# A four-layer graph network in split fp32: twelve SBUF tensors laid 32 bytes off the 64-byte multiples

## The chip, the cores and the metric

The kernel runs on one core of one Trainium2 chip. The metric is the device time of one execution in microseconds (us). The profile gives one execution, instruction by instruction, on the core's engines: PE (TensorE matrix products) and PEld (its loads of the stationary operand), DVE (VectorE), ACT (ScalarE), POOL (GpSimd) and SP (which issues the transfers).

## What is computed

Thirty-two graphs of 256 nodes with 256 features go through four layers, each followed by a residual sum and a layer norm. The parts that matter here:

```python
def _L0_gnn_ref(x, in_mat, out_mat, w3_w, ...):      # in_mat = out_mat = adj
    for _ in range(3):
        a_in = jnp.einsum('nm,bmd->bnd', in_mat, h)
        av = jnp.concatenate([a_in, a_out], axis=-1)
        z = sigmoid(_lin(av, w3_w, w3_b) + _lin(h, u3_w, u3_b))
        r = sigmoid(_lin(av, w4_w, w4_b) + _lin(h, u3_w, u3_b))
        hv = tanh(_lin(av, w5_w, w5_b) + _lin(r * h, u5_w, u5_b))
        h = (1.0 - z) * h + z * hv
def _L1_gnn_ref(s, adjacency, Wq, Wk, Wv):           # relation, masked and normed, times values
    rel = adjacency.T[None] * jnp.einsum('bnd,bmd->bnm', q, k)
    return jnp.einsum('bnm,bmd->bnd', rel / norm(rel, axis=2, keepdims=True), v)
def _L2_gnn_ref(x, adj, weight, bias):   # (adj x) W + b
def _L3_gnn_ref(x, adj, weight, bias):   # (D^-1/2 adj D^-1/2)(x W) + b
x = _layernorm(x + L0(x)); x = _layernorm(x + L1(x)); x = _layernorm(x + L2(x)); x = _layernorm(x + L3(x))
```

## The kernel before

Two graphs are one pair; there are 16 pairs. A full tile is 128 partitions x 2 x 512 numbers of four bytes: features on the partitions, the nodes of both graphs along the row. Every operand of a product is kept as two tensors of type fp32r, the rounded value (`_hi`) and the rest (`_lo`), and each product is three: high by high, high by low, low by high. So each matrix is a `Split` of two tensors.

The products come in two shapes. In the **512-column** products a weight matrix is the stationary operand (128 of its columns) and 512 columns of a state tile move through the array: `base` (u3T), `reset` (w4T), `update` (w34T), `candidate_mixed` (w5T), `candidate_reset` (u5T). In the **256-column** products a matrix or tile of 256 columns moves:

- `mix` and `mix_nodes`: `adjT` (or `norm_adjT`) moves, the stationary operand is 128 columns of a node-major state (`hf_node`, `hb_node`, `b_a`).
- `convolve`: `w2s` or `w3s` moves, `b_rh` is stationary.
- `keys`: the split sum (`sum_hi`, `sum_lo`) moves, `wqk` is stationary.
- `values`: `wvT` moves, the split sum is stationary.
- `relate`: the keys (`b_rh`) move, the split sum is stationary.
- `attend`: the values (`v_hi`, `v_lo`) move, the split relation (`rel_hi`, `rel_lo`) is stationary.

In the profile a product is written out<-moving,stationary, so `b_ps<-sum_hi,wqk_lo` has the high half of the sum moving over `wqk_lo`. Each product is a load of 128 stationary columns (PEld) and the matmul (PE). Line 515 is the call in the helper `matmul`, line 510 that in `product`.

The order of work on every engine is written out by hand: a part for the start, a loop body that PE, DVE, ACT, POOL and SP run 13 times, and an ending in which the last two pairs run side by side. A body works on two recurrence steps of the front pair (`f_`, `hf_`), the third step of the pair before it (`b_`, `hb_`), and that pair's other three layers. Engines meet through semaphores. The last pair (`last_pair`) has no tensors of its own: its sum stands in `hb_feat_hi` and `hb_feat_lo`, its relation in `hf_node_hi` and `hf_node_lo`, its values in `hf_feat_hi` and `hf_feat_lo`.

Tensors are laid out in SBUF in the order in which they are allocated, each start rounded up to 32 bytes. In the built program of before, all operands of all products start at multiples of 128 bytes: `adjT_hi` at 16512, `wqk_hi` at 49280, `b_rh_hi` at 155264, `sum_hi` at 190080, `rel_hi` at 214656. Slices of them start at multiples of 512 bytes from there. Some small tensors and `bias_out` (at 64928, read by DVE at line 1715) already stand 32 bytes off a multiple of 64.

The lines that allocate what the change moves:

```python
        def split_matrix(name):
            return Split(sb(name + "_hi", [P, C, D], F32R), sb(name + "_lo", [P, C, D], F32R))

        adjT = split_matrix("adjT")
        norm_adjT = split_matrix("norm_adjT")
```

Of the kernel before, what the change touches and what calls it, by code (L numbers as in the profile page):

```python
# [21 lines left out]
P = 128  # L22
F32 = mybir.dt.float32
F32R = mybir.dt.float32r
# [136 lines left out]
def build(nc, x, adj, w3_w, w3_b, u3_w, u3_b, w4_w, w4_b, w5_w, w5_b, u5_w, u5_b, wq, wk, wv,  # L161
          l2_w, l2_b, l3_w, l3_b, out):
    B, N, D = x.shape
    C = N // P
    G = 2
    T = G * N
# [9 lines left out]
    with ExitStack() as ctx:  # L176
        def sb(name, shape, dt=F32):
            return ctx.enter_context(nc.sbuf_tensor(name, shape, dt))
# [5 lines left out]
        def split_matrix(name):  # L184
            return Split(sb(name + "_hi", [P, C, D], F32R), sb(name + "_lo", [P, C, D], F32R))

        adjT = split_matrix("adjT")
        norm_adjT = split_matrix("norm_adjT")
        w34T = split_matrix("w34T")
        w4T = split_matrix("w4T")  # L190
        w5T = split_matrix("w5T")
# [1 line left out]
        u5T = split_matrix("u5T")  # L193
        wvT = split_matrix("wvT")
        wqk = split_matrix("wqk")
        w2s = split_matrix("w2s")
        w3s = split_matrix("w3s")

        ident = sb("ident", [P, P])
        adj_nat = sb("adj_nat", [P, C, N])  # L200
# [47 lines left out]
        def nodes(name, dt=F32):  # L248
            return sb(name, [P, G, C, D], dt)

        main = Layers(sb, sem, "b", back, per_graph, input_t, s_input_t, 0,
                      (sb("sum_hi", [P, C, T], F32R), sb("sum_lo", [P, C, T], F32R)), nodes("normed"), nodes("result"),
                      (nodes("v_hi", F32R), nodes("v_lo", F32R)), (nodes("rel_hi", F32R), nodes("rel_lo", F32R)),
                      sb("sq_sum", [P, G, N]), True)


# [1981 lines left out]
```

## Time and profile before

| | us |
|---|---|
| median of 3 runs | 1224.64 |
| lowest and highest | 1224.62, 1224.92 |
| the profiled execution | 1224.91 |
| its span, first to last instruction | 1223.1 |
| outside the span | 1.8 |

The profiled execution stands 0.27 us over the median of the runs. Its mean granted TensorE clock was 0.998 of full speed. The profile's page gives busy time by engine, 40 slices of the span, the chain of work that ended last and the costliest groups of instructions; views of the trace give instructions in order of time, groups by line and tile, and busy time by stretch. A matmul's recorded length includes its way through the array and overlaps the next one's, so what a matmul costs in a run is the distance from its start to the next start, not its length.

### The profile page before, as it was taken

To read this page: it belongs to the slowest core of one execution; us is meant where nothing else is said; L and a number is where in the kernel's file an instruction comes from. 1 tells how busy PE (TensorE), PEld (TensorE's weight loads), DVE (VectorE), ACT (ScalarE), POOL (GpSimd) and SP (SyncE) were. 2 spreads that over 40 slices of the span, in tenths; PEclk is the share of its full clock that TensorE was granted. 3 is DMA by queue.
4 is the path that set the end of the run, shared out by engine and by line. 5 is a ranking of instruction groups with operands and counts; after the bars stand their busy time and mean duration, and the time that the engine had idled before them with its cause. 6 is when DMAs were issued, how large, how long until landed. Compare 5 with 4: busy or idle time off the path is not lost.

```text
span 1223.1 us, 21243 instructions
## 1 busy us (share of the span) xinstructions
PE 1207.9 (99%) x7454; PEld 1089.1 (89%) x7454; DVE 1003.4 (82%) x2220; ACT 657.5 (54%) x1179; POOL 192.8 (16%) x447
## 2 busy tenths in 40 slices
PE   9999999999999999999999999999999999999997
PEld 7789899898998989899898998989989898998896
DVE  7689788897878978788887888978789787886799
ACT  5455555555555555555555555555555555555542
POOL 1002021110211102012020211102111021120122
PEclk9999999999999999999999999999999999999999
DMA  6020221303113030120402213031130311300001
GB/s 207 18 84 21 63 77 35 103 0 86 51 34 103 0 103 34 46 91 1 119 17 53 84 34 103 0 86 51 34 103 0 103 34 42 95 1 35 1 2 35
DMA packets 105021, 66.93 MB, mean 55 GB/s; under 512 B 65690, under 2 KB 98468, under 8 KB 104996
## 3 DMA queue, kind: packets, MB, share of 16 engines
q1 hardware_dynamic: 104784, 66.08, 18.2%
q0 software_dynamic: 192, 0.52, 0.2%
q8 instruction: 15, 0.25, 0.1%
q14 instruction: 10, 0.08, 0.0%
q10 hardware_dynamic: 20, 0.01, 0.0%
HBM read 35.13 MB, written 23.07 MB: 48 GB/s over the span
## 4 chain that ended last, share of the span: by engine, by line
PE 97%; DVE 2%; POOL 0%; ACT 0%; issue 0%; DVEq 0%; POOLq 0%
PE b_ps L515 41%; PE f_ps L515 31%; PE f_ps L510 15%; PE b_ps L510 7%; PE f_ps L677 1%; PE b_ps L741 1%; PE b_ps L559 0%; PE f_ps L1052 0%; DVE b_stats L1678 0%; DVE f_stats L1678 0%; DVE f_gate L1694 0%; PE b_ps L574 0%; DVE hf_feat L1706 0%; DVE hf_feat L1694 0%; DVE normed L1694 0%
## 5 line engine op out<-in xcount | busy, mean ns | idle before, releaser
L423 POOL TENSOR_TENSOR b_var_eps<-b_moments,eps 128x2 f32<-128x2 f32 x120 | 34.9, 290 | 913.1 <-DVE b_moments L1685 913.0
L1115 ACT ACTIVATE f_cand<-f_ps,bias_c 128x512 f32<-128x512 f32 x66 | 45.6, 691 | 86.0 <-PE f_ps L515 84.3
L425 POOL TENSOR_TENSOR b_rstd<-b_var_eps,neg_half 128x2 f32<-128x2 f32 x120 | 88.2, 735 | 9.4
L1063 ACT ACTIVATE b_rh_hi<-b_ps 128x512 fp32r<-128x512 f32 x90 | 53.7, 596 | 65.5 <-PE b_ps L515 65.5
L1103 ACT ACTIVATE f_gate<-f_ps,bias_r 128x512 f32<-128x512 f32 x66 | 45.4, 688 | 70.7 <-PE f_ps L515 70.7
L1063 ACT ACTIVATE b_a_hi<-normed 128x512 fp32r<-128x512 f32 x60 | 37.9, 632 | 61.3 <-DVE normed L1694 61.3
L515 PE MATMUL f_ps<-adjT_hi,hf_node_hi 128*128 128x256 f32 x264 | 67.3, 287 | 0.5 <-DVE adjT_lo L1481 0.5
L515 PE MATMUL f_ps<-adjT_lo,hf_node_hi 128*128 128x256 f32 x264 | 66.1, 283 | 0.0
L1720 DVE TENSOR_TENSOR b_rh_lo<-b_ps,b_rh_hi 128x512 fp32r<-128x512 f32 x90 | 61.4, 682 | 4.6 <-ACT b_rh_hi L1063 4.4
L1577 DVE TENSOR_TENSOR f_cand<-f_z,f_cand 128x512 f32<-128x512 f32 x66 | 45.5, 689 | 23.0 <-ACT f_cand L1115 23.0
L1561 DVE TENSOR_TENSOR f_gate<-f_gate,hf_feat 128x512 f32<-128x512 f32 x66 | 44.8, 680 | 20.2 <-ACT f_gate L1103 20.2
L1063 ACT ACTIVATE f_a_hi<-f_ps 128x512 fp32r<-128x512 f32 x66 | 39.0, 592 | 40.5 <-PE f_ps L515 40.5
L1555 DVE TENSOR_TENSOR b_a_lo<-b_ps,b_a_hi 128x512 fp32r<-128x512 f32 x30 | 19.4, 687 | 49.2 <-ACT b_a_hi L1063 49.2
L1111 ACT ACTIVATE f_z<-f_ps,bias_z 128x512 f32<-128x512 f32 x66 | 45.1, 685 | 26.6 <-PE f_ps L510 26.6
L1555 DVE TENSOR_TENSOR f_a_lo<-f_ps,f_a_hi 128x512 fp32r<-128x512 f32 x66 | 44.9, 682 | 14.0 <-ACT f_a_hi L1063 14.0
L1182 ACT ACTIVATE result<-result,b_shift,b_rstd 128x256 f32<-128x256 f32 x56 | 30.8, 597 | 46.2 <-POOL b_shift L431 46.2
L1063 ACT ACTIVATE hf_feat_hi<-hf_feat 128x512 fp32r<-128x512 f32 x64 | 38.8, 626 | 25.1 <-DVE hf_feat L1641 22.2
L515 PE MATMUL f_ps<-hf_feat_hi,u3T_hi 128*128 128x512 f32 x132 | 52.0, 394 | 0.1
L515 PE MATMUL f_ps<-f_a_hi,w4T_hi 128*128 128x512 f32 x132 | 51.8, 393 | 0.0
L515 PE MATMUL f_ps<-hf_feat_hi,u3T_lo 128*128 128x512 f32 x132 | 51.8, 392 | 0.0
L515 PE MATMUL f_ps<-f_a_hi,w4T_lo 128*128 128x512 f32 x132 | 51.6, 391 | 0.0
L510 PE MATMUL f_ps<-f_a_hi,w34T_hi 128*128 128x512 f32 x132 | 51.5, 390 | 0.0
(340 smaller groups left out, 4335.7 us busy)
## 6 DMA issues: line engine op xcount, KB each, us to landing
x_front<-in_x SPq DMA_DIRECT2D x16, 512.0 KB, 4.0
x_blocks<-in_x SPq DMA_DIRECT2D x60, 128.0 KB, 2.9
input_t<-hf_feat SPq DMA_DIRECT2D x15, 512.0 KB, 2.9
turn_sum<-normed SPq DMA_DIRECT2D x14, 512.0 KB, 2.7
result<-turn_sum SPq DMA_DIRECT2D x56, 128.0 KB, 2.8
turn_f<-f_gate SPq DMA_DIRECT2D x14, 512.0 KB, 2.7
f_z<-turn_f SPq DMA_DIRECT2D x56, 128.0 KB, 2.8
out<-result SPq DMA_DIRECT2D x14, 512.0 KB, 3.2
```

Of the source, the lines that this page charges most:

```text
L423: pool.tensor_tensor(Y.var_eps[:, g], Y.moments[:, g, :, 1], eps[:], ALU.add).then_inc(Y.s_var, 1)
L425: pool.tensor_tensor(Y.rstd[:, g], Y.var_eps[:, g], neg_half[:], ALU.pow).then_inc(Y.s_rstd, 1)
L510: last = pe.matmul(bank, s, m, start=start and i == 0, stop=stop and i == len(terms) - 1, skip_group_check=True)
L515: return pe.matmul(bank, s, m, start=start, stop=stop, skip_group_check=True)
L1063: return act.activation(dst, src, ACT.Copy)
L1103: act.activation(L.gate[:, k], L.ps0[:, k], ACT.Sigmoid, bias=bias_r[:, k:k + 1]).then_inc(L.s_r, 1)
L1111: act.activation(L.z[:, k], L.ps0[:, k], ACT.Sigmoid, bias=bias_z[:, k:k + 1]).then_inc(L.s_z, 1)
L1115: act.activation(L.cand[:, k], L.ps1[:, k], ACT.Tanh, bias=bias_c[:, k:k + 1]).then_inc(L.s_tanh, 1)
L1555: dve.tensor_tensor(L.a_lo[:, k], L.ps1[:, k], full(L.a_hi[:, k]), ALU.subtract).then_inc(L.s_a_lo, 1)
L1561: dve.tensor_tensor(L.gate[:, k], L.gate[:, k], L.state.feat[:, k], ALU.mult).then_inc(L.s_rh, 1)
L1577: dve.tensor_tensor(L.cand[:, k], L.z[:, k], L.cand[:, k], ALU.mult).then_inc(L.s_zc, 1)
L1720: dve.tensor_tensor(lo[:, g], src, full(hi[:, g]), ALU.subtract).then_inc(done, 1)
```

## The change

Twelve tensors (four split matrices, the split sum and the split relation) are allocated behind a new tensor of 32 bytes, and a second one of 32 bytes follows them, so that all that comes behind stands where it stood relative to 64. The order of instructions on all five engines is word for word that of before, with the same shapes; what differs is addresses alone.

In the built program after, these twelve tensors start 32 bytes off a multiple of 64: `adjT_hi` (173728), `adjT_lo`, `norm_adjT_hi`, `norm_adjT_lo`, `w2s_hi`, `w2s_lo`, `w3s_hi`, `w3s_lo`, `sum_hi` (190112), `sum_lo`, `rel_hi` (198304), `rel_lo`. All the other operands of products keep their place relative to 64.

```diff
-        adjT = split_matrix("adjT")
-        norm_adjT = split_matrix("norm_adjT")
...
-        w2s = split_matrix("w2s")
-        w3s = split_matrix("w3s")
...
+        shift_32 = sb("shift_32", [P, 8])
+        adjT = split_matrix("adjT")
+        norm_adjT = split_matrix("norm_adjT")
+        w2s = split_matrix("w2s")
+        w3s = split_matrix("w3s")
+        sum_split = sb("sum_hi", [P, C, T], F32R), sb("sum_lo", [P, C, T], F32R)
+        rel_split = nodes("rel_hi", F32R), nodes("rel_lo", F32R)
+        shift_back = sb("shift_back", [P, 8])
+
         main = Layers(sb, sem, "b", back, per_graph, input_t, s_input_t, 0,
-                      (sb("sum_hi", [P, C, T], F32R), sb("sum_lo", [P, C, T], F32R)), nodes("normed"), nodes("result"),
-                      (nodes("v_hi", F32R), nodes("v_lo", F32R)), (nodes("rel_hi", F32R), nodes("rel_lo", F32R)),
+                      sum_split, nodes("normed"), nodes("result"),
+                      (nodes("v_hi", F32R), nodes("v_lo", F32R)), rel_split,
                       sb("sq_sum", [P, G, N]), True)
```

So in each 256-column product of the first fifteen pairs exactly one of the two operands stands off by 32 bytes: the moving one in `mix`, `mix_nodes`, `convolve` and `keys`, the stationary one in `values`, `relate` and `attend`. In the 512-column products neither does, nor in the last pair's `keys`, `values`, `relate` and `attend`.

## Rows read from the trace of the kernel before

**Rows 1.** The page: engines' busy time, granted clock, and the chain that ended last.

```profile
PE 1207.9 (99%) x7454; PEld 1089.1 (89%) x7454; DVE 1003.4 (82%) x2220; ACT 657.5 (54%) x1179; POOL 192.8 (16%) x447
...
PEclk9999999999999999999999999999999999999999
...
PE 97%; DVE 2%; POOL 0%; ACT 0%; issue 0%; DVEq 0%; POOLq 0%
```

**Rows 2.** Busy time by stretch: start and length, then each engine (x instructions), clock, DMA.

```profile
0.00:54.00 54.00, 49.23 (x255) 41.80 (x256) 39.06 (x75) 29.50 (x49) 4.25 (x15) 0.97 0.42 127
...
572.65:647.00 74.35, 74.35 (x462) 67.19 (x461) 61.64 (x136) 40.94 (x76) 11.91 (x28) 1.00 0.19 56
...
1093.10:1223.10 130.00, 119.61 (x770) 108.13 (x768) 104.74 (x253) 57.26 (x102) 23.30 (x48) 0.99 0.05 17
```

**Rows 3.** Chain that ended last, in order of time: start us, length us, what.

```profile
592.20 5.44 PE f_ps L515 x24
605.80 7.19 PE b_ps L515 x60
652.93 5.47 PE b_ps L515 x24
658.40 5.44 PE b_ps L510 x24
```

**Rows 4.** PE in order of time, from 512 to 256 columns: start us, length us, instruction.

```profile
602.92 0.39 PE L510 MATMUL f_ps<-f_a_hi,w34T_hi 128*128 128x512 f32 x1
...
605.19 0.62 PE L515 MATMUL f_ps<-f_rh_lo,u5T_hi 128*128 128x512 f32 x2
605.64 0.28 PE L515 MATMUL b_ps<-sum_hi,wqk_hi 128*128 128x256 f32 x1
605.75 0.28 PE L515 MATMUL b_ps<-sum_hi,wqk_lo 128*128 128x256 f32 x1
605.87 0.28 PE L515 MATMUL b_ps<-sum_hi,wqk_hi 128*128 128x256 f32 x1
...
607.07 0.28 PE L515 MATMUL b_ps<-sum_hi,wqk_hi 128*128 128x256 f32 x1
```

**Rows 5.** PE in order of time, 512-column matmuls right behind a 256-column run.

```profile
629.23 0.40 PE L510 MATMUL f_ps<-f_a_hi,w34T_hi 128*128 128x512 f32 x1
629.46 0.40 PE L510 MATMUL f_ps<-f_a_lo,w34T_hi 128*128 128x512 f32 x1
629.70 0.39 PE L510 MATMUL f_ps<-f_a_hi,w34T_lo 128*128 128x512 f32 x1
...
630.62 0.28 PE L515 MATMUL b_ps<-adjT_hi,b_a_hi 128*128 128x256 f32 x1
```

**Rows 6.** PEld in order of time: weight loads of eight 128-column transposes, then the next.

```profile
644.61 0.90 PEld L677 LDWEIGHTS f_ps<-ident,hb_feat 128*128 128x128 f32 x8
645.47 0.19 PEld L515 LDWEIGHTS b_ps<-w3s_hi,b_rh_hi 128*128 128x128 f32 x1
```

**Rows 7.** Groups by line: out<-moving,stationary, x count | busy us, mean ns | idle before.

```profile
L515 PE MATMUL f_ps<-adjT_hi,hf_node_hi 128*128 128x256 f32 x264 | 67.3, 287 | 0.5 <-DVE adjT_lo L1481 0.5
...
L510 PE MATMUL f_ps<-f_a_hi,w34T_lo 128*128 128x512 f32 x132 | 51.3, 389 | 0.0
...
L515 PE MATMUL b_ps<-sum_hi,wqk_lo 128*128 128x256 f32 x120 | 30.1, 283 | 0.0
...
L515 PE MATMUL f_ps<-hb_feat_hi,wqk_hi 128*128 128x256 f32 x8 | 2.0, 283 | 0.0
...
L510 PEld LDWEIGHTS f_ps<-f_a_hi,w34T_lo 128*128 128x128 f32 x132 | 24.8, 188 | 5.3
...
L515 PEld LDWEIGHTS b_ps<-sum_hi,wqk_lo 128*128 128x128 f32 x120 | 23.0, 191 | 0.6
```

**Rows 8.** One tile each: count, duration ns min/median/max, first and last start us.

```profile
L1715 DVE TENSOR_TENSOR b_ps<-normed,bias_out x60: 674/694/700, 105.4 to 1212.9; 128x512 f32<-128x512 f32 x60
L1724 DVE TENSOR_TENSOR sum_lo<-b_cand,sum_hi x30: 676/686/690, 78.0 to 1158.2; 128x512 fp32r<-128x512 f32 x30
```

**Rows 9.** DVE and PE in order of time at a hand-over in a body (`mix_nodes` to `convolve`).

```profile
642.89 0.69 DVE L1720 TENSOR_TENSOR b_rh_lo<-b_ps,b_rh_hi 128x512 fp32r<-128x512 f32 x1
643.27 0.28 PE L515 MATMUL b_ps<-w3s_hi,b_rh_hi 128*128 128x256 f32 x1
...
644.23 0.28 PE L515 MATMUL b_ps<-w3s_hi,b_rh_lo 128*128 128x256 f32 x1
```

## Prediction, made before the changed kernel was run

> **What bounds the kernel now.** The first view is the page's: PE is busy in 99% of the span, its clock is granted in full in every slice, and the chain that ended last lies 97% on PE [rows 1]. That busy share alone says little, since matmuls overlap in the records. So the second view is busy time by stretch: in one loop body of 74.35 us PE is busy in all of it and never waits, DVE is busy in 61.64 us (83%), ACT in 40.94 [rows 2]. Thirteen such bodies are 967 of the 1223.1 us. PE is the bound, and no other engine holds it up there; only the start and the ending, with 49.23 busy of 54.00 and 119.61 of 130.00 us, have gaps [rows 2].
>
> The third view is what a matmul costs by its distance to the next. The chain's pieces give it best: 24 matmuls of 512 columns take 5.44 us, 226.7 ns each, and 60 of 256 columns (`keys`, `values(0)` and `relate`) take 7.19 us, 119.8 ns each [rows 3]. By single starts it is the same: ten 512-column steps from 602.92 to 605.19 are 2.27 us, ten 256-column steps from 605.87 to 607.07 are 1.20 us [rows 4]. Here the two shapes do not agree. At 226.7 ns for 512 columns, 256 columns should take 113.3 ns. They take 120, so 6.7 ns of each are not moving columns.
>
> **Where the 6.7 ns sit.** The first 256-column matmul behind a 512-column run takes only 0.11 us (605.64 to 605.75), the next ones 0.12 [rows 4]. It has the same operands, the same addresses modulo 64 and the same shape; what differs is how its stream lies in time against the load of the next weights. The other side of the same thing: 512-column matmuls right behind a 256-column run start at 629.23, 629.46 and 629.70 and six of them take 1.39 us, 232 ns each and up to 0.24, against 226.7 later [rows 5]. The weight load is recorded at 191 ns under 256 columns and 188 under 512, the 256-column matmul at 283 [rows 7]. So a load and a stream that run together can cost more or less, at the same addresses, by their relative position, and the steady state of a 256-column run is the dear one. Could it be the weight load alone that sets 120 ns? Eight loads for 128-column transposes start within 0.86 us, 107.5 ns apart [rows 6]. These are a transpose's loads, so this bounds the load rather than measures it, but it leaves room under 113.3.
>
> **The change part by part.** Instructions, their order and their shapes are the same on all engines; no wait, transfer or queue moves. What can change is the time of an instruction that reads or writes one of the twelve tensors.
>
> *PE.* The 256-column matmuls number 4224: three groups like the first of x264, 27 groups of x120, 24 groups of x8 in the last pair [rows 7]. Of the last pair's, twelve groups (96 matmuls) touch no moved tensor. In the other 4128 the two operands were in step modulo 64 and are now 32 bytes apart. That is an untried relation: no product in the trace has it, so it has to be bounded. Below: the load at 107.5 ns, 12.5 ns less per matmul, if the shift also took away what both shapes pay now [rows 6]. Above: the dearest step of the 512-column rows, 0.24 us, 13 ns over 226.7 [rows 5]; on the same footing a 256-column step would cost 113.3 + 13 = 126, 6 ns more than now. The nearest row is the 0.11 us step, since it is the same matmul with another relative position [rows 4]. A shift by 32 bytes is eight numbers of the stream, 8 x 0.443 = 3.5 ns of it at the 512-column rate (226.7 / 512). The relation moves by a few ns, as it does between the first matmul of a run and the rest. I take 113.3 for that reason. It is a choice: the row shows that position matters, not that this position is the good one.
>
> Not all 4128 pay 6.7 ns now. The first one or two of a run are already cheap, and some sit behind a wait. I count nine in ten, 3,700: 3,700 x 6.7 ns = **24.8 us**.
>
> *512-column products.* None of their operands moves, and they are 2880, fifteen groups of x132 and fifteen of x60, such as the one shown [rows 7]. What they pay behind a 256-column run, (232 - 226.7) x 6 = 32 ns [rows 5], should go if that run ends in the cheap relation. With about ten such places in each of some 15 passes this is at most 4.8 us. I take half, **2.4 us**.
>
> *DVE, ACT and the transfers.* DVE writes `sum_lo` at 32 bytes off now. The trace has such a case: `bias_out` stands off already, and the DVE operation that reads it takes 694 ns against 686 for `sum_lo` with the same shape, and that difference includes a PSUM destination [rows 8]. At 8 ns for the 60 `sum_lo` and `rel_lo` writes it is 0.5 us in all, on an engine that is idle for 12.7 us of each body [rows 2]; zero. On ACT it is likewise off the path.
>
> *What is late next.* A body would shrink by about 1.8 us to 72.6, with DVE at 61.64, 85%. Hand-overs inside it: `b_rh_lo` is written by 643.58 and first read at 644.23, 0.65 us of slack [rows 9]. Between the matmuls that feed it and that read lie some 20 of 256 columns, which shrink by 0.13 us. So in the body the whole gain stays. In the ending, where PE lacks 10.4 of 130 us [rows 2], about 600 of the matmuls stand, worth 3.6 us, and I give half of that back, and 1.5 us for the start and for new short waits: **-3.3 us**.
>
> The sum: 24.8 + 2.4 - 3.3 = 23.9 us. The profiled execution took 1224.91, so 1201.0; the median before is 0.27 lower, and I forecast **1201 us**.
>
> A page that speaks against this: the Trainium skill, "TensorE: Matmul & The Clock Gate", section "Step-by-step: what each phase is for", says PE has two independent SBUF read ports, so that loading the next weights steals no bandwidth from the running matmul. "SBUF — State Buffer", section "Specifications (TRN2)", gives lines of 16 bytes, and 32 is a multiple of 16, so both streams would cross as many lines as before. By both rules the sum is zero and the time 1224.6. The first rule does not sit well with 0.11 and 0.12 us for the same matmul [rows 4]; the second no row here tests.
>
> **The rivals.**
>
> *Nothing moves.* The 6.7 ns are the cost of swapping weights at this pace, a chain from the start of one matmul to the load it lets go and back, and addresses play no part. For it: it also explains why only the first of a run is cheap, since its weights were loaded long before. Against it: it doesn't explain why 512-column matmuls, whose loads end early, take three or more steps to get from 0.23-0.24 back to 0.227 [rows 5]. Time: 1224.6. By the page's rules above this is the outcome, and it has a chance of 0.26.
>
> *Half of it moves.* The stream has to be displaced, not the weights. Then `values`, `relate` and `attend` (72 of a body's 264) keep 120 ns, and the rest gains: 192/264 x 23.9 = 17.4, 1207. If it is the other way round, 6.5 us and 1218. Together 0.13.
>
> *The wrong way.* A run always settles where load and stream hold each other up; the shift only moves the point where they settle, and 32 bytes apart it is dearer. It decides from 0.6 ns a matmul on (0.6 x 4128 = 2.5 us). The place is each steady 256-column run of the body, and PE has no cover there [rows 2]. The mid of its bound, 3 ns on 4128, is 12 us: 1237; at the 6 ns bound 1249. At one lost step of 0.9 ns (two columns' time) it is 3.7 us and 1228. Chance 0.18.
>
> *More than the rest.* Runs come down to the load's 107.5 ns: 12.5 x 3,700 = 46 us, 1179 less what new waits take back, about 1183. Chance 0.03.
>
> **How the numbers follow.** Forecast 0.40; half 0.13; nothing 0.26; wrong way 0.18; more 0.03. A measurement of this kernel tells 0.2%, 2.4 us, from no change. Faster: 0.40 + 0.13 + 0.03 = 0.56; same 0.26; slower 0.18. The likeliest case's own range is 1196 to 1206 (113.3 reached by 3,400 to 4,128 of them, and the give-back from 1 to 5 us). The range of 8 in 10 must take in nothing, half and the small end of the wrong way: 1196 to 1236. It leaves out 0.03 and some 0.04 below and 0.10 above.
>
> **What would show each step.** After the change the piece of 60 matmuls that took 7.19 us should take 6.8; ten steps of `keys` 1.13 us instead of 1.20; the recorded length of a 256-column matmul 278 or less instead of 283; pieces of 24 of 512 columns stay at 5.44. A body should take 72.6 us instead of 74.35. If `keys`, `mix` and `convolve` change and `values`, `relate` and `attend` do not, the half case holds. If every distance is still 0.12, addresses play no part. I would be wrong, with the mechanism right, if the matmuls come down but PE begins to wait on DVE in the body.

## The result: 9.9 us faster, 14 us less than forecast

| | before | after |
|---|---|---|
| median, us | 1224.78 (1224.62 to 1224.98) | 1214.85 (1213.32 to 1216.14) |
| profiled execution, us | 1224.91 | 1214.77 |
| its span, us | 1223.1 | 1212.9 |
| loop body, us | 74.35 | 73.69 |

The ratio is 0.9918, with a 95% interval from 0.9902 to 0.9934. The time lies inside the range of the forecast and on its likeliest side, but the gain is 9.9 us where 23.6 (1224.64 - 1201) was named. The line numbers of after are 5 higher: L515 is L520, L510 is L515, L1720 is L1725.

The page of after, against [rows 1]: PE still busy in 99%, and 97% of the chain is on it.

```profile
PE 1198.3 (99%) x7454; PEld 1079.2 (89%) x7454; DVE 1002.6 (83%) x2220; ACT 655.7 (54%) x1179; POOL 191.7 (16%) x447
...
PE 97%; DVE 2%; POOL 0%; ACT 0%; issue 0%; DVEq 0%; POOLq 0%
```

Busy time by stretch of after, columns as in [rows 2]: the start, one body, the ending.

```profile
0.00:54.00 54.00, 49.70 (x263) 42.37 (x264) 39.92 (x76) 29.49 (x49) 4.24 (x15) 1.00 0.41 127
...
572.60:646.29 73.69, 73.69 (x462) 66.49 (x461) 61.58 (x136) 40.86 (x74) 11.89 (x29) 1.00 0.19 57
...
1083.00:1212.90 129.90, 119.60 (x765) 108.14 (x764) 104.45 (x253) 56.48 (x101) 22.53 (x48) 0.97 0.05 17
```

PE is busy in all of the body, as before, and the work of DVE and ACT in it is the same to 0.1 us. A body is 0.66 us shorter; thirteen are 8.6 of the 10.2 us by which the spans differ. Up to the loop after is 2.2 us ahead, and behind the loop it loses 0.7 again. TensorE's granted clock has a part in both: in each of the two profiled executions it falls once from 2.4 to 1.2 GHz ahead of PE's last matmuls, in the start of before and in the ending of after. A stretch of each, columns as above:

```profile
50.00:53.00 3.00, 3.00 (x10) 2.51 (x11) 1.83 (x3) 0.71 (x2) 0.00 (x0) 0.50 0.01 3
```

```profile
1182.00:1185.00 3.00, 3.00 (x16) 3.00 (x16) 3.00 (x12) 0.00 (x0) 0.59 (x2) 0.50 0.00 0
```

Ahead of the fall PE had waited: it was busy in 1.7 of the 3.9 us up to 49.9 in before, and in 2.0 of the 3.7 us up to 1181.7 in after. `e1_matrices` below waits as long at both places (busy in 1.7 of 3.9 and 2.0 of 3.7 us) and its clock stays at 1.00, so what decides is not in these rows. The fall costs before 1.6 us: from the matmul at 45.02 to the one at 57.24 are 12.22 us, and in `e6_by_256` below, a kernel with the same steps whose clock does not fall there, the same two are 10.65 us apart (44.66 and 55.31). `e2_sum_rel`, `e3_by_64`, `e4_conv_64` and `e7_also_512` have one such fall too, `e1_matrices`, `e5_chosen` and `e6_by_256` none before PE's last matmuls. So a difference of 1 to 2 us between two executions can be the clock alone, and the length of a body, which none of these falls touches, is the finer measure.

The chain of after in order of time (start us, length us), against [rows 3].

```profile
572.43 5.46 PE b_ps L520 x24
577.89 5.44 PE b_ps L515 x24
...
599.65 7.07 PE b_ps L520 x60
```

The 60 matmuls of `keys`, `values(0)` and `relate` take 7.07 us where they took 7.19, or 117.8 ns each where 119.8 were; the forecast was 6.8. The 24 of 512 columns take 5.44 us as before. By the time from each start to the next, without the few of over 0.28 us, 4,221 steps of 256 columns come to 501.7 us (118.87 ns each) against 4,223 and 511.4 (121.09; short waits are in both means), and the 512-column steps of up to 0.3 us average 227.8 against 227.6 ns. So the 256-column matmuls lost 9.7 us and nothing else moved by more than a fraction of that.

PE in order of time, after: `keys`, as in [rows 4], the first matmul of `relate`, and a 512-column run right behind 256 columns, as in [rows 5].

```profile
599.60 0.28 PE L520 MATMUL b_ps<-sum_hi,wqk_lo 128*128 128x256 f32 x1
...
600.89 0.28 PE L520 MATMUL b_ps<-sum_hi,wqk_hi 128*128 128x256 f32 x1
...
603.71 0.28 PE L520 MATMUL b_ps<-b_rh_hi,sum_hi 128*128 128x256 f32 x1
...
606.55 0.40 PE L520 MATMUL f_ps<-hf_feat_hi,u3T_hi 128*128 128x512 f32 x1
...
607.48 0.62 PE L520 MATMUL f_ps<-hf_feat_lo,u3T_hi 128*128 128x512 f32 x2
607.95 0.28 PE L520 MATMUL b_ps<-wvT_hi,sum_hi 128*128 128x256 f32 x1
```

Eleven steps of `keys` are 1.29 us, 117 ns each; 24 of `relate`, from 603.71 to 606.55, are 2.84 us, 118 ns each. The six 512-column matmuls take 1.40 us, 233 ns each, where [rows 5] had 232: what they pay on entering did not go.

Groups of after, against those of [rows 7]: the recorded lengths went from 283 to 278 ns, and the load from 192 to 189 for `adjT_lo` over `hf_node_hi`.

```profile
L520 PE MATMUL b_ps<-sum_hi,wqk_lo 128*128 128x256 f32 x120 | 29.3, 278 | 0.0
...
L520 PEld LDWEIGHTS f_ps<-adjT_lo,hf_node_hi 128*128 128x128 f32 x264 | 49.9, 189 | 0.2
```

Inside one body of after, the steps by product (means over runs of 12 or 24 starts, without the three runs whose first step is 0.20 us in both kernels) sort by the distance of the two operands. In what follows the *distance* is the start of the moving operand minus that of the stationary one, modulo 256 bytes, and a *settled* step is the mean once a run is past its first few matmuls.

| product | distance before | ns | distance after | ns |
|---|---|---|---|---|
| `mix`, `mix_nodes`, `convolve`, `keys`: moving one shifted | 0 | 120 | 32 | 116.7 to 116.9 |
| `values`, `relate`: stationary one shifted | 0 | 120 | 224 | 118.2 to 118.5 |
| `attend` (the values now stand at 64) | 0 | 120 | 32 | 117.0 |

`attend` has its stationary side shifted like `values` and `relate`, but goes with the products at distance 32. So no shift reaches 113.3. The questions for the runs were: is it really the relation of the two addresses, what is its rule, and why 116.7 and not 113.3?

### The profile page after: what moved, and what is told of

It is laid out like the page before. It is cut to its first block, busy times and chain, and to the rows that moved or that the text cites. A ratio compares the mean times of both kernels' runs of the same rounds, so it can differ in the third digit from the quotient of the medians.

```text
span 1212.9 us, 21243 instructions
## 1 busy us (share of the span) xinstructions
PE 1198.3 (99%) x7454; PEld 1079.2 (89%) x7454; DVE 1002.6 (83%) x2220; ACT 655.7 (54%) x1179; POOL 191.7 (16%) x447
## 4 chain that ended last, share of the span: by engine, by line
PE 97%; DVE 2%; POOL 0%; ACT 0%; issue 0%; DVEq 0%; POOLq 0%
PE b_ps L520 41%; PE f_ps L520 32%; PE f_ps L515 15%; PE b_ps L515 7%; PE f_ps L682 1%; PE b_ps L746 1%; PE b_ps L564 0%; PE f_ps L1057 0%; DVE f_stats L1683 0%; DVE hf_feat L1699 0%; DVE f_gate L1699 0%; DVE b_rh_lo L1725 0%; PE b_ps L579 0%; DVE b_ps L1720 0%; PE f_ps L589 0%
## 5 line engine op out<-in xcount | busy, mean ns | idle before, releaser
L520 PE MATMUL f_ps<-adjT_hi,hf_node_hi 128*128 128x256 f32 x264 | 66.4, 285 | 0.0
L520 PE MATMUL f_ps<-adjT_lo,hf_node_hi 128*128 128x256 f32 x264 | 65.0, 280 | 0.0
L1725 DVE TENSOR_TENSOR b_rh_lo<-b_ps,b_rh_hi 128x512 fp32r<-128x512 f32 x90 | 61.1, 679 | 4.0 <-ACT b_rh_hi L1068 3.9
L520 PE MATMUL f_ps<-hf_feat_hi,u3T_hi 128*128 128x512 f32 x132 | 52.3, 396 | 0.2 <-DVE u3T_lo L1486 0.2
L520 PE MATMUL f_ps<-f_a_hi,w4T_hi 128*128 128x512 f32 x132 | 51.9, 393 | 0.0
L520 PE MATMUL f_ps<-hf_feat_hi,u3T_lo 128*128 128x512 f32 x132 | 51.7, 391 | 0.0
L515 PE MATMUL f_ps<-f_a_lo,w34T_hi 128*128 128x512 f32 x132 | 51.5, 390 | 0.0
L520 PE MATMUL f_ps<-f_rh_hi,u5T_lo 128*128 128x512 f32 x132 | 51.5, 390 | 0.0
```

The source lines that it names most:

```text
L515: last = pe.matmul(bank, s, m, start=start and i == 0, stop=stop and i == len(terms) - 1, skip_group_check=True)
L520: return pe.matmul(bank, s, m, start=start, stop=stop, skip_group_check=True)
L1725: dve.tensor_tensor(lo[:, g], src, full(hi[:, g]), ALU.subtract).then_inc(done, 1)
```

## The experiments

### One distance after the other, on PE alone

`m1_offsets` leaves the network out and runs only loads and matmuls: eight of 512 columns, then 36 of 256 columns at one pair of offsets, eighteen pairs in a row.

```
+MOVING = {"mva": 0, "mvb": 16, "mvc": 32, "mvd": 48, "mve": 64, "mvf": 96, "mvg": 128, "mvh": 8, "mvi": 256}
+STATION = {"sta": 0, "stb": 16, "stc": 32, "std": 48, "ste": 64, "stf": 128}
```

> It leaves the network out: PE alone runs 36 matmuls of 256 columns per case, each behind eight of 512 columns, with the moving and the stationary operand at set distances from a multiple of 512 bytes, and five runs of 24 matmuls of 512 columns. Theory A, the relation of the two start addresses modulo 64 sets the cost: with both at 0, 120 ns a matmul as in the kernel before; 32 bytes apart, either way round, about 116.7 ns as in the settled runs of the changed kernel; 64, 128 and 256 apart as at 0; both at 32 as at 0. Theory B, what counts is that an operand itself stands off, whatever the other does: both at 32 is then the cheap one too or cheaper still. Theory C, the 6.7 ns are a chain of weight swaps and the gain came from a side of the layout: all cases near 120 ns. 512 columns: 226.7 ns in every case by A and C.

PE in order of time (start us, length us of the whole group). The start of the next group less that of this one, by 36, is the mean step.

```profile
34.11 4.36 PE L83 MATMUL ps<-mvc,sta 128*128 128x256 f32 x36
38.31 2.00 PE L83 MATMUL ps<-mva,sta 128*128 128x512 f32 x8
...
70.69 4.47 PE L83 MATMUL ps<-mvi,sta 128*128 128x256 f32 x36
75.01 2.00 PE L83 MATMUL ps<-mva,sta 128*128 128x512 f32 x8
...
89.11 4.42 PE L83 MATMUL ps<-mva,stc 128*128 128x256 f32 x36
93.37 2.01 PE L83 MATMUL ps<-mva,sta 128*128 128x512 f32 x8
...
113.58 4.47 PE L83 MATMUL ps<-mvc,stc 128*128 128x256 f32 x36
117.89 1.99 PE L83 MATMUL ps<-mva,sta 128*128 128x512 f32 x8
...
136.16 5.65 PE L83 MATMUL ps<-mva,sta 128*128 128x512 f32 x24
141.65 5.77 PE L83 MATMUL ps<-mvc,sta 128*128 128x512 f32 x24
147.26 5.71 PE L83 MATMUL ps<-mvb,sta 128*128 128x512 f32 x24
```

The moving operand 32 off: 4.20 us for 36 (116.7 ns). 64 off: 117.8 by its starts. 256 off: 4.32 (120.0), as at 0. The stationary one 32 off: 4.26 (118.3). Both 32 off: 4.31, back at 120. So the relation counts, and in these cases neither address by itself. No other engine ran, so DVE, ACT and the transfers have no part in it. The theory that the period is 64 bytes falls at once: 64 is nearly as good as 32. Three readings don't fit a pure distance: both operands 16 off gives 116.7, not 120; 16 against 32 (117.3) differs from 0 against 16 (118.2); and the stationary operand 128 off gives 120.1 where the moving one 128 off gives 118.6, though modulo 256 the distance is the same. Whether absolute places count too or these cases settled differently (see `m3_entries`) stays open; no operand of the kernel stands 16 bytes off.

The 512-column matmuls go the other way: 24 of them take 5.49 us at distance 0 and 5.61 at 32, entry included (once settled, 226.7 and 233.3 ns a step).

### The two halves of the change

`e1_matrices` shifts only the four matrices by 32 bytes; everything behind them stands at 64.

```
         w3s = split_matrix("w3s")
+        shift_back = sb("shift_back", [P, 8])
         sum_split = sb("sum_hi", [P, C, T], F32R), sb("sum_lo", [P, C, T], F32R)
         rel_split = nodes("rel_hi", F32R), nodes("rel_lo", F32R)
-        shift_back = sb("shift_back", [P, 8])
```

> Only adjT, norm_adjT, w2s and w3s stand off by 32 bytes; sum and relation are back on a multiple of 64. Theory A: mix, mix_nodes and convolve keep their gain (168 of a body's 264 matmuls), keys, values, relate and attend lose it: 9.9 x 168/264 = 6.3 us of gain, 1218.5 us. A rival, that the whole gain belongs to the relation of the sum and relation tiles: 1224.8 us.

It measured 1212.65 us (1212.06 to 1213.26), ratio 0.9902 with an interval from 0.9886 to 0.9917: with less of the change done it is as fast or faster (in the median by 2.2 us, by the bodies, 73.60 us against 73.69, by 1.2; the profiled execution of after has a fall of the clock and this one's none). The edit was meant to undo one part and did something else: it put sum and relation at 64, not back in step. Distances became 64 in `keys`, 192 in `values` and `relate`, 0 in `attend`.

PE in order of time, `e1_matrices`: `relate`, the product that had 118.2 ns in after.

```profile
602.76 0.28 PE L520 MATMUL b_ps<-b_rh_hi,sum_hi 128*128 128x256 f32 x1
...
604.12 0.28 PE L520 MATMUL b_ps<-b_rh_hi,sum_hi 128*128 128x256 f32 x1
...
605.48 0.40 PE L520 MATMUL f_ps<-hf_feat_hi,u3T_hi 128*128 128x512 f32 x1
```

From 602.76 to 605.48 are 24 starts: 113.3 ns each. That is the step forecast, and the 60 matmuls of the chain take 6.92 us. So 113.3 can be had, but not at 32 bytes. `values(0)` goes from 122 to 113 within its first four matmuls and has 114.3; `values(1)`, the same product at the same addresses behind a 512-column run, has 117.8.

`e2_sum_rel` shifts only sum and relation by 32.

```
-        shift_32 = sb("shift_32", [P, 8])
         adjT = split_matrix("adjT")
...
         w3s = split_matrix("w3s")
+        shift_32 = sb("shift_32", [P, 8])
         sum_split = sb("sum_hi", [P, C, T], F32R), sb("sum_lo", [P, C, T], F32R)
```

> Only the split sum and the split relation stand off by 32 bytes. Theory A: keys, values, relate and attend gain (96 of 264): 9.9 x 96/264 = 3.6 us, 1221.2 us; the two halves add up to the whole change. If the halves don't add up, the runs influence each other. Rival: 1214.9 us, all of the gain is here.

It measured 1221.68 us (nine runs, 1221.33 to 1222.75), ratio 0.9975 with an interval from 0.9965 to 0.9985. Its chain shows the 60 matmuls and the 36 of `mix_nodes` and `convolve`:

```profile
604.34 7.07 PE b_ps L520 x60
...
629.08 4.31 PE b_ps L520 x36
```

The 60 are at 7.07 us, as in after; the 36 at 4.31 (119.8 ns each), as in before, where after has 4.20. So each part acts on its own products and only there, and the part on sum and relation is worth about a third of the change.

### The period

`e3_by_64` shifts the same tensors by 64 bytes, `e6_by_256` by 256.

```
-        shift_32 = sb("shift_32", [P, 8])
+        shift_32 = sb("shift_32", [P, 16])
...
-        shift_back = sb("shift_back", [P, 8])
+        shift_back = sb("shift_back", [P, 16])
```

In `e6_by_256` the same two lines have 64 instead of 16.

> As the change, with 64 bytes in place of 32. Theory A, modulo 64: nothing is left, 1224.8 us, 120 ns a matmul. If the pattern repeats only after 128 bytes or more, a time other than that of before, and perhaps the 113 ns that the prediction counted on (1201 us).

> As the change, with 256 bytes in place of 32 on both sides. If what counts is the distance modulo 256, all matmuls are back at 120 ns and the time is that of before, 1224.8 us. If it is that the tensors stand elsewhere in SBUF at all, or in another order, the gain stays: 1214.9 us.

`e3_by_64`: 1215.14 us (1213.98 to 1215.38), 0.9917 (0.9903 to 0.9930), the same gain as by 32. `e6_by_256`: 1224.97 (eleven runs, 1223.00 to 1226.26), 1.0001 (0.9992 to 1.0010), nothing.

The chain of `e3_by_64` and then that of `e6_by_256`, from the same place in a body.

```profile
600.81 6.92 PE b_ps L520 x60
...
625.40 4.25 PE b_ps L520 x36
```

```profile
603.94 7.19 PE b_ps L520 x60
...
628.92 4.31 PE b_ps L520 x36
```

By 64 the run of 60 is cheaper than in after (6.92), and `mix_nodes` with `convolve` dearer (4.25 us for 36, 118 ns, where after has 4.20). By 256 both are where they were before. This run has all tensors moved and allocated as in the change, so neither the order of allocation nor the place in SBUF at large does anything; the distance modulo 256 does.

### One settled cost for each distance, or several?

After `e1_matrices` two theories were left. *By distance alone*: each distance has its step, and 192 has 113.3. *Several settled states*: at one distance a run may settle at different steps, and what ran before chooses. `m2_products` (the network left out again) takes distances from 0 to 320 in the kernel's own two patterns of operands, each behind eight 512-column matmuls.

```
+MOVING = {"mva": 0, "mvb": 32, "mvc": 64, "mvd": 96, "mve": 128, "mvf": 160, "mvg": 192, "mvh": 224, "mvi": 320}
+STATION = {"sta": 0, "stc": 64}
```

> It leaves the network out and runs matmuls alone, in the kernel's own two patterns: one stationary under two moving operands (mix, convolve, values, attend), then one moving operand over two stationary ones (keys, relate), 36 matmuls of 256 columns per distance, and 24 of 512 columns per distance. Theory D, the cost is set by the distance moving minus stationary, modulo 256 bytes, and by the pattern: distance 0 gives 120 in both patterns; 32 about 116.7; 320 as 64; moving at 0 over stationary at 64 as distance 192; both at 64 as 0; one moving operand over two stationary ones at distance 192 gives 113.7, as relate in the run of the four matrices alone. Theory E, absolute places count: the pairs with equal distance differ by over 1 ns. 512 columns: 226.7 at distance 0 and 231 to 233 at 32 by both, since the first run of this kind showed that; open for the others.

The chain, the pieces of 36 of 256 columns at distances 32, 64, 96 and 192 (between them stand eight of 512).

```profile
30.99 4.20 PE ps L94 x36
...
37.03 4.24 PE ps L94 x36
...
43.13 4.32 PE ps L94 x36
...
61.51 4.24 PE ps L94 x36
```

Settled steps by distance behind the eight of 512 columns, the same in both patterns to 0.1 ns:

| distance, bytes | 0 | 32 | 64 | 96 | 128 | 160 | 192 | 224 | 320 |
|---|---|---|---|---|---|---|---|---|---|
| 256 columns, ns | 120.0 | 116.7 | 117.8 | 120.0 | 118.6 | 118.7 | 117.8 | 118.3 | 117.8 |
| 512 columns, ns | 226.7 | 233.3 | 228.9 | 233.3 | 233.3 | 234.6 | 233.3 | 233.3 | 228.6 |

320 equals 64, and the stationary operand 64 off equals 192. But 192 gives 117.8 here and never 113.3. The theory by distance alone is refuted for `relate` of `e1_matrices`.

`m3_entries` (network left out) puts, behind the eight of 512 columns, twelve of 256 at a first distance and then 24 at a second.

```
+            for first in ("mva", "mvb", "mvc", "mvg", "mve", "mvh"):
+                for then in MOVING:
+                    wide("mva", "sta", 8)
+                    by_station(first, "sta")
+                    by_station(then, "sta")
+                    by_station(then, "sta")
```

> It leaves the network out. Six distances (0, 32, 64, 192, 128, 224 bytes, moving minus stationary) run for 12 matmuls of 256 columns behind eight of 512, then each of eight distances for 24. Theory F, one distance has more than one settled state and the run before chooses: behind 64 the distance 192 settles at 113.3 ns, as values and relate do in the run of the four matrices alone, and behind 512-column matmuls or behind 192 itself at 117.8. Theory D, the distance alone sets the cost: 24 matmuls of one distance cost the same behind every entry, within 0.5 ns, and the 113.3 in values and relate have another cause. By both, distance 0 stays at 120.

PE in order of time; `mva` stands at 0, `mvb` at 32, `mvc` at 64, `mvg` at 192.

```profile
60.86 2.90 PE L93 MATMUL ps<-mvg,sta 128*128 128x256 f32 x24
63.60 0.63 PE L88 MATMUL ps<-mva,sta 128*128 128x512 f32 x2
...
83.68 1.56 PE L93 MATMUL ps<-mvb,sta 128*128 128x256 f32 x12
85.08 2.88 PE L93 MATMUL ps<-mvc,sta 128*128 128x256 f32 x24
87.80 2.00 PE L88 MATMUL ps<-mva,sta 128*128 128x512 f32 x8
...
156.66 1.58 PE L93 MATMUL ps<-mvc,sta 128*128 128x256 f32 x12
158.07 2.99 PE L93 MATMUL ps<-mvg,sta 128*128 128x256 f32 x24
160.90 0.62 PE L88 MATMUL ps<-mva,sta 128*128 128x512 f32 x2
```

At 64 bytes, behind twelve at 32, 24 matmuls take 2.72 us, 113.3 ns each; behind 64, the same addresses settle at 117.7. At 192 bytes, behind 0, the last eleven have 113.4 (2.74 us for 24 with the entry); behind 64 or 192 they have 117.7 (2.83 us). At 64 the cheap step came behind 32 alone, at 192 behind 0 alone, of six entries each. Other distances have two steps as well: 32 settles at 116.7 behind five entries and at 117.8 behind 0, 128 at 118.6 behind five and at 120.0 behind 224, and 160 at 117.3 behind three and 118.8 behind the other three. Only 0 and 96 (both 120.0) and 224 (118.3) settle at the same step behind all six. So one distance can have several settled steps, and the run before chooses. The case named ahead of it, 192 behind 64, did not come here though the kernel shows it: the choice depends on more than the two distances. (This run has only the pattern of one stationary operand under two moving ones; `keys` and `relate` have the other.) Which relation at the entry leads where stays open.

### Using it

`e4_conv_64` is `e1_matrices` with `w2s` and `w3s` at 64 instead of 32, so that `convolve` follows `mix_nodes` (at 32) at 64.

```
         norm_adjT = split_matrix("norm_adjT")
+        shift_back = sb("shift_back", [P, 8])
         w2s = split_matrix("w2s")
```

> As the run of the four matrices alone (1212.65 us), but w2s and w3s stand 64 bytes off where adjT and norm_adjT stand 32 off, so that convolve (distance 64) follows mix_nodes (distance 32). Theory F, two settled states and the run before chooses: 36 of a body's 48 convolve matmuls go from 116.7 to 113.3 ns, the 12 behind the transposes from 116.7 to 117.8: 0.11 us less a body, 1211.0 us. Theory D, distance alone: convolve at 117.8, 0.05 us more a body, 1213.4 us.

It measured 1212.64 us (1211.97 to 1213.54), 0.9900 (0.9885 to 0.9915), the same as `e1_matrices`: between the two expectations and undecided by its time. The trace says why. The half of the second `convolve` right behind `mix_nodes` has 113.6 ns, as expected. The first `convolve` has 118.0, the other state, where `e1_matrices` had 116.7. Ahead of the second the run of `mix_nodes` is even; ahead of the first a load comes late. All engines in order of time, `e4_conv_64`:

```profile
624.83 0.68 DVE L1725 TENSOR_TENSOR b_a_lo<-normed,b_a_hi 128x512 fp32r<-128x512 f32 x1
...
625.55 0.28 PE L520 MATMUL b_ps<-adjT_lo,b_a_hi 128*128 128x256 f32 x1
625.57 0.54 PEld L520 LDWEIGHTS b_ps<-adjT_hi,b_a_lo 128*128 128x128 f32 x4
...
626.15 0.28 PE L520 MATMUL b_ps<-w2s_hi,b_rh_hi 128*128 128x256 f32 x1
```

DVE has `b_a_lo` done at 625.51, and its first load starts at 625.57, some 20 ns behind the matmul under which it would lie. The steps there are 121 and 125 ns in an otherwise even run of 117. That this entry chose the state of the 24 behind it is what the theory would say; no run took the late load away. In a body 12 matmuls won 3.2 ns each, 24 lost 1.3 and the 12 behind the transposes lost 1.1, which cancels: the body takes 73.60 us in both.

`e5_chosen` sets two more distances by these findings: the front's node-major state 32 bytes down, so that `mix` of the front follows `mix` of the back (at 32) at 64, and the relation at 32 again.

```
+        if by_blocks:
+            self.node_before = sb(f"{name}_node_before", [P, 56])
         self.node_hi, self.node_lo = sb(f"{name}_node_hi", by_graph, F32R), sb(f"{name}_node_lo", by_graph, F32R)
+        if by_blocks:
+            self.node_behind = sb(f"{name}_node_behind", [P, 8])
...
         norm_adjT = split_matrix("norm_adjT")
+        rel_split = nodes("rel_hi", F32R), nodes("rel_lo", F32R)
         shift_back = sb("shift_back", [P, 8])
```

> As the one before, and hf_node stands 32 bytes before a multiple of 256 off the others (distance 64 in the front mix, behind distance 32 in the back mix), and the relation 32 bytes off (distance 32 in attend in place of 0). Theory F: front mix behind back mix 113.3 in place of 116.7 (24 matmuls), the other front mix 117.8 in place of 116.7 (24), attend 116.7 in place of 119 (24): another 0.1 us less a body, 1209.5 us, below both kernels. Theory D: front mix 117.8 throughout, 1213.5 us.

The chain of `e5_chosen`: the front's `mix` (24), the 60 of `keys`, `values(0)` and `relate`, `mix_nodes` with half of `convolve` (36).

```profile
567.90 2.72 PE f_ps L524 x24
...
597.89 6.92 PE b_ps L524 x60
...
632.14 4.16 PE b_ps L524 x36
```

It measured a median of 1212.03 us (1210.38 to 1212.52, and one far outlier of 6611; without it the median is 1211.75), 0.9897 (0.9882 to 0.9912), where 1209.5 and 1213.5 were expected; the profiled execution took 1210.38. The front's `mix` behind the back's has 113.5 ns (2.72 us for 24; after has 116.7), `attend` 116.8. It is the fastest version, 2.8 us below after, with the same instructions. Against `e1_matrices` it is 0.6 us better in the median, less than the spread of either. The traces show more: the body is 0.11 us shorter (73.49 against 73.60), 1.4 us over thirteen, and the two profiled executions, both without a fall of the clock, took 1210.38 and 1212.06.

### Does the same shift help 512 columns?

`e7_also_512` is the change, and also moves the five weight matrices of the 512-column products (`w34T`, `w4T`, `w5T`, `u3T`, `u5T`), the stationary side there, by 32 bytes.

```
-        w34T = split_matrix("w34T")
...
-        u5T = split_matrix("u5T")
...
         w3s = split_matrix("w3s")
+        w34T = split_matrix("w34T")
...
+        u5T = split_matrix("u5T")
```

> As the change, and the weights of the 512-column products (w34T, w4T, w5T, u3T, u5T) stand 32 bytes off as well. The bare run gave 233.3 ns in place of 226.7 for 512 columns at distance 32: 2880 x 6.6 = 19 us more, 1234 us. If the prediction's idea held for 512 columns too, that 32 bytes apart is the cheaper relation, the time would be at or below 1214.9.

It measured 1230.32 us (1230.10 to 1230.43), 1.0046 (1.0032 to 1.0060): slower than before, and 15.5 us slower than after. Its chain has 24 of 512 columns at

```profile
581.05 5.60 PE b_ps L520 x24
...
609.05 7.06 PE b_ps L520 x60
```

5.60 us instead of 5.44, 233.3 ns each, with the 256-column runs as in after. All 512-column steps together rose by 15.7 us (651.2 in before, 666.9 here). That is less than the 19 us expected, because it counted 6.6 ns for all 2880 while those behind a 256-column run were dear already: the mean rose from 227.6 to 233.2. The weights are the stationary side, so the distance here is 224, which has 233.3 in the table too. Distance 0, the dear one for 256 columns, is the cheap one for 512.

## Why the prediction was right in its sign and wrong in its size

*PE bounds the kernel, the body has no cover.* Right. A body is busy on PE from end to end in both traces, and what the matmuls lose the time loses: 9.7 us of steps, 9.9 of median. The clock was not granted in full throughout, as the prediction has it: the start has 0.97 in [rows 2], and the page's tenths don't show so short a fall. The forecast does not hang on it.

*Load and stream hold each other up by their relative addresses.* That the relative addresses set the step is right, and now shown: in step 120.0 ns, 32 apart 116.7, both 32 off 120.0 again, 256 apart 120.0 again, with nothing but PE running, and 1224.97 us for the kernel shifted by 256. "Nothing moves" is refuted. That the load and the stream hold each other up is how the prediction reads this, and it fits; no run took the loads away or moved them in time, so it is not shown. The Trainium skill says in "TensorE: Matmul & The Clock Gate", section "Step-by-step: what each phase is for", that loading the next weights takes no read bandwidth from the running matmul, the two having ports of their own. By that the distance should make no difference, and here it makes one of 3.3 ns. By the 16-byte lines that the Trainium skill gives in "SBUF — State Buffer", section "Specifications (TRN2)", a shift by 32 should be neutral too, and it is not. Why, no run shows.

*"I take 113.3 for that reason."* This is the step that failed, and nearly the whole miss. The forecast took 6.7 ns off each of 3,700 matmuls. Measured, the 192 of a body whose moving side is shifted lost 3.3 ns at most, the others 1.5 to 3. A body gained 0.66 us over its 264 matmuls, 2.5 ns each, where 1.8 us were forecast; the steps of the whole run gained 9.7 us instead of 24.8. The reason given, that the nearest row is the 0.11 us step of the first matmul, was a weak one. In `m1_offsets` at distance 0 the steps behind a 512-column run are 113, 119, 120, 120 and so on, and at distance 32, behind the same run, 119, 117, 117, 116. So a short first step goes with a dear settled one here, and a long first step with a cheap one: the first step says nothing about where a run settles. The second argument, that 32 bytes move the relation by 3.5 ns, gave a direction and no size. The cost over the distance isn't monotone, and a settled 113.3 was seen only at 64 and 192 bytes behind certain runs. Why 32 bytes settle at 116.7 stays open.

*The count.* Nine in ten of 4,128 was a side issue: with 3.3 and 1.8 ns in place of 6.7 the difference between 3,700 and 4,128 is under 1.5 us.

*512-column entries, 2.4 us.* Wrong. They cost the same as before (233 ns each over six, against 232).

*New waits and the give-back, 3.3 us.* Not there. The start has 4.3 us without PE where it had 4.8, the ending 10.3 where it had 10.4 [rows 2]. With two fifths of the gain the question of what is late next never came up. The two terms, 2.4 and -3.3, nearly cancel, so neither makes the miss.

*DVE at zero.* Right: 61.58 us in a body against 61.64.

*The rivals.* "Half of it moves" had a question with something in it, which side is displaced: with the moving side shifted a matmul gains 3.3 ns, with the stationary one 1.5 to 1.8 in `values` and `relate`. But both gain, and `attend` (3.0) shows that it is the distance, 32 or 224, and not the side. "The wrong way" named a mechanism that is real: a relation 32 bytes apart, either way round, is dearer in the settled state, for 512 columns, by 6.6 ns. Had the change moved one of those operands too, it would have come out slower, as `e7_also_512` did. The likeliest case's own range, 1196 to 1206, took in neither a step between 113.3 and 120 nor a difference between the products; 116.7 lies midway between the two known steps, and nothing in the trace of before favoured either over the middle. With the mid of 120 and 113.3 on 3,700 the sum would have been 12.4 + 2.4 - 3.3 = 11.5 us, and the time 1213. That this is so near is in part luck, since 12.4 is over the 9.7 measured and the two small terms were not there.

## What to carry to other kernels

Where PE is the bound and each matmul has its own weight load, look at the step between starts against the columns it moves, and compare two shapes: a surplus in one of them (here 6.7 ns at 256 columns) may hang on the distance of the two operands' addresses modulo 256 bytes, which costs next to nothing to change. Measure the distances for the shape in a bare loop first, since the best one differs by shape: here it is 32 bytes for 256 columns, or 64 behind a run at 32, and 0 for 512. Then look at the steps in the kernel itself, since the bare loop did not foretell `relate`: 117.8 ns there, 113.3 in the kernel. And where an effect has two known ends and no row says which holds, forecast the middle and put both ends in the range.

## What the runs showed that was not expected

- The start distance of the two operands modulo 256 bytes sets the settled step of fp32r matmuls with a load each, behind the same run: 116.7 to 120.0 ns at 256 columns, 226.7 to 234.6 at 512, with opposite signs at 32 bytes (-3.3 and +6.6 ns).
- The same instructions at the same addresses can settle at 113.3 or 117.8 ns (256 columns, 64 or 192 bytes apart), by what ran before them. At 32, 128 and 160 bytes too there are two settled steps, 1 to 1.5 ns apart.
- With both operands 16 bytes off the step is 116.7, though the distance is 0; so the distance isn't all of it.
- Executions of the kernel before lie some 3 us apart (1222.98 to 1226.26). In the traces one fall of the granted clock from 2.4 to 1.2 GHz, near 50 us or at 1182 us, is worth some 1.6 us; six of the nine traces of the whole kernel have it and three don't.
